# A four-stage transformer kernel on one core: the experts' low-rank product in float32r parts, keys in two transfers, and new orders on every engine

## The reference

```
x = layernorm(x + attention0(x))   # 16 heads, q and k low-rank, causal softmax
x = layernorm(x + ffn0(x))         # silu(x w1) * (x w2), gelu(h h1), gelu(h h2), w3; hidden 512
x = layernorm(x + attention1(x))   # 16 heads, no mask
x = layernorm(x + experts(x))      # below
```

```
top1 = argmax(softmax(x @ gate_W.T + gate_b))          # one of 8 experts per token
base = x @ wi_W.T + wi_b                               # 128 -> 512, shared
lora = (x @ lora_A[i].T) @ lora_B[i].T                 # 128 -> 4 -> 512, expert i
out  = sum over i of (top1 == i) * (relu(base + lora) @ wo_W.T + wo_b)
```

## Time and profile before

| | us |
|---|---|
| median of three runs | 875.84 (875.03 to 881.42) |
| the profiled execution, its own time | 876.6 |
| its span, first to last instruction | 874.5 |
| PE busy | 823.0 |
| DVE busy | 611.2 |
| ACT busy | 402.6 |
| POOL busy | 190.5 |
| mean granted clock of PE | 0.958 |

### The profile page before, as it was taken

One profiled execution on the slowest core, in us unless ns is written; L12 is line 12 of the kernel. 1 busy time (PEld: TensorE's weight loads), 2 busy tenths in 40 slices (PEclk: granted clock), 3 DMA queues, 4 the chain that ended last, 5 costly groups with the idle time before them and its releaser, 6 DMA issues.

```text
span 874.5 us, 21713 instructions
## 1 busy us (share of the span) xinstructions
PE 823.0 (94%) x8690; PEld 626.7 (72%) x8690; DVE 611.2 (70%) x1715; ACT 402.6 (46%) x823; POOL 190.5 (22%) x398
## 2 busy tenths in 40 slices
PE   8679999999989999999999999999999899999885
PEld 6457776777767687877778786877778677777554
DVE  3574685968668587877768786848847784847554
ACT  1323536273643736273554628182463627371441
POOL 4332421130302122131313113040211314010001
PEclk9789899999999999999999999999889999999779
DMA  6522222201330221213240302313020400111200
GB/s 217 203 85 74 85 87 76 75 27 61 119 121 4 87 73 37 82 56 106 68 153 21 128 32 65 104 50 112 4 92 15 141 4 27 55 36 46 87 9 13
DMA packets 43468, 64.19 MB, mean 73 GB/s; under 512 B 6088, under 2 KB 34088, under 8 KB 42984
## 3 DMA queue, kind: packets, MB, share of 16 engines
q1 hardware_dynamic: 41688, 57.93, 20.2%
q10 hardware_dynamic: 1680, 4.87, 1.6%
HBM read 43.41 MB, written 18.35 MB: 71 GB/s over the span
## 4 chain that ended last, share of the span: by engine, by line
PE 75%; DVE 7%; ACT 5%; DMA 4%; SPq 4%; issue 3%; POOL 2%; POOLq 0%; DVEq 0%; ACTq 0%
PE banks L1116 25%; PE banks L1065 10%; PE banks L1098 6%; PE banks L1172 6%; PE banks L976 5%; PE banks L1032 5%; ACT prob L618 3%; DVE top L741 3%; PE banks L943 3%; PE banks L1145 3%; DMA krow<-scratch 2%; PE banks L1077 2%; SPq L480 2%; PE banks L952 2%; PE banks L1047 2%
## 5 line engine op out<-in xcount | busy, mean ns | idle before, releaser
L741 DVE TENSOR_REDUCE top<-banks 128x3 f32<-128x384 f32 (+1 forms) x512 | 290.0, 613 | 72.7 <-PE banks L983 50.4
L618 ACT ACTIVATE prob<-banks 128x384 f32<-128x384 f32 (+1 forms) x512 | 242.0, 560 | 91.6 <-PE banks L1040 43.1
L632 ACT ACTIVATE hid<-banks 128x512 f32<-128x512 f32 x64 | 38.1, 597 | 237.0 <-PE banks L1116 237.0
L555 POOL TENSOR_TENSOR ln_rstd<-ln_var,minus_half 128x2 f32<-128x2 f32 x64 | 44.5, 701 | 439.7 <-DVE ln_var L820 439.4
L1065 PE MATMUL banks<-prob,v 128*32 128x256 f32 (+1 forms) x2048 | 122.0, 373 | 7.7 <-POOL prob L562 4.6
L1116 PE MATMUL banks<-glu,wh 128*128 128x256 f32 x512 | 120.3, 389 | 0.0
L1116 PE MATMUL banks<-hid,wh 128*128 128x256 f32 x512 | 119.3, 387 | 0.1
L1116 PEld LDWEIGHTS banks<-glu,wh 128*128 128x128 f32 x512 | 96.7, 194 | 15.6 <-issue 1.0
L1116 PEld LDWEIGHTS banks<-hid,wh 128*128 128x128 f32 x512 | 96.1, 193 | 13.9 <-DVE top L741 0.4
L1065 PEld LDWEIGHTS banks<-prob,v 128*32 128x32 f32 x2048 | 59.3, 113 | 53.0 <-issue 11.5
L976 PE MATMUL banks<-krow,qrow 32*128 32x256 f32 (+1 forms) x992 | 76.9, 336 | 14.8 <-DMA krow<-scratch 10.8
(11 more groups left out here) (110 smaller groups left out, 1027.1 us busy)
## 6 DMA issues: line engine op xcount, KB each, us to landing
scratch<-split SPq DMA_DIRECT2D x124, 128.0 KB, 2.2
qrow<-scratch SPq DMA_DIRECT2D x31, 512.0 KB, 3.6
krow<-scratch SPq DMA_DIRECT2D x124, 128.0 KB, 3.2
xt<-in_xt SPq DMA_DIRECT2D x16, 128.0 KB, 2.6
wh<-in_wh ACTq DMA_DIRECT2D x2, 1024.0 KB, 7.7
out<-xout SPq DMA_DIRECT2D x16, 128.0 KB, 2.1
x<-in_x SPq DMA_DIRECT2D x15, 128.0 KB, 3.0
prob<-in_qk_a SPq DMA_DIRECT2D x2, 512.0 KB, 4.9
```

The source lines that it names most:

```text
L555: nc.gpsimd.tensor_tensor(ln_rstd[s][:], ln_var[s][:], minus_half[:], ALU.pow).then_inc(rstd[s], 1)
L618: nc.scalar.activation(prob[s][:, j % 2, g, 0:wide], banks[:, b, 0:wide], ACT.Exp, scale=1.0 / float(np.sqrt(np.float32(HD))) if s == A0 e ...
L632: nc.scalar.activation(hid[layer][:, 2 * m:2 * m + 2, :].rearrange("p m t -> p (m t)"), banks[:, g, :], ACT.Gelu).then_inc(gelued, 1)
L741: nc.vector.tensor_reduce(out=top[s][:, :, h], in_=banks[:, b, 0:blocks * wide].rearrange("p (q k) -> p q k", q=blocks), axis=AX, op=ALU.m ...
```

## The change

Six edits; the line numbers behind `route` shift by up to 13 in the new file.

1. The low-rank product: `low` now holds, for each tile of 128 tokens, 4 x 32 columns. DVE rounds the 32 columns to float32r (`low_parts[0]`), takes the rest (`low_parts[1]`), and writes both masked, twice over. lora_B is loaded four times and made into parts as well (once, in chunk 0's route): `wlb` is its float32r value on rows 0 to 63 and the rest on rows 64 to 127. One float32r product over 128 rows then gives all four products of parts.
2. `exp_full` counts pairs of hidden blocks, and ACT's relu waits per pair.
3. The keys of a fetch come in two transfers of 256 KB, each writing a row twice, instead of four of 128 KB.
4. The last `late` step waits for `folded` (its landing place is one that the start uses), and loads lora_B four times.
5. POOL no longer clears `low`.
6. `SEQUENCE` of all five engines and `BANK_TABLE` are new.

```diff
-        NSPREAD = (1 + PARTS * PARTS) * DMA
+        NSPREAD = (1 + PARTS) * DMA
...
-        NWEIGHTS = 8 * DMA
+        NWEIGHTS = (6 + PARTS * PARTS) * DMA
         NSCALED = 5
+        ROUTED = 9
...
-                for i in range(PARTS):
-                    for k in range(PARTS):
-                        sp.dma_start(krow[s][n % DEEP[s]][PARTS * i + k::PARTS * PARTS].bitcast(F32).rearrange("p j t -> p (j t)"),
-                                     scratch[s][n % 2][1, :, k]).then_inc(there, DMA)
+                for k in range(PARTS):
+                    sp.dma_start(krow[s][n % DEEP[s]][k::PARTS].bitcast(F32).rearrange("p j t -> p (j t)"),
+                                 scratch[s][n % 2][1, :, k].unsqueeze(1).to_broadcast([GROUP * HD, PARTS, GROUPS * TOK])).then_inc(there, DMA)
...
+                    act.wait_ge(folded, 2)
                     for dst, name in ((wq[A1][:], "qk_w1"), (wv[A1][:], "v_w1"), (wo[A1][:], "o_w1"), (wi[:], "wi"), (wgl[:], "gl"),
-                                      (wlb[0:ER], "lb"), (wlb[ER:2 * ER], "lb"), (wout[:], "wo")):
+                                      *((lbraw[i * ER:(i + 1) * ER], "lb") for i in range(PARTS * PARTS)), (wout[:], "wo")):
...
-                act.wait_ge(exp_full, 1 * n + 1)
                 for pair, g in enumerate((ga, gb)):
+                    act.wait_ge(exp_full, PAIRS * n + pair + 1)
...
+                if is_first(n):
+                    dve.wait_ge(weights, NWEIGHTS)
+                    nc.vector.tensor_copy(wlb[:], lbraw).then_inc(lb_parts, 1)
+                    dve.wait_ge(lb_parts, 1)
+                    at = slice(PARTS * ER, P)
+                    nc.vector.tensor_tensor(wlb[at], lbraw[at], wlb[at].bitcast(F32), ALU.subtract).then_inc(lb_parts, 1)
...
+                nc.vector.tensor_copy(low_parts[:, :, 0].bitcast(F32R), src[:, :, EXPERTS:]).then_inc(routed, 1)
+                step(2, nc.vector.tensor_tensor(logit[:], src[:, :, 0:EXPERTS], row("gate_b").unsqueeze(1).to_broadcast(wide), ALU.add))
+                nc.vector.tensor_tensor(low_parts[:, :, 1], src[:, :, EXPERTS:], low_parts[:, :, 0], ALU.subtract).then_inc(routed, 1)
...
+                step(8, nc.vector.tensor_tensor(chosen[:].rearrange("p t (e r) -> p t e r", r=LORA), pick[:].unsqueeze(3).to_broadcast(wider),
+                                                first[:].unsqueeze(2).unsqueeze(3).to_broadcast(wider), ALU.is_equal))
+
+                for k in range(PARTS):
+                    done = nc.vector.tensor_tensor(low[:, :, k].rearrange("p t (i c) -> p t i c", i=PARTS), low_parts[:],
+                                                   chosen[:].unsqueeze(2).to_broadcast([P, TILES, PARTS, ER]), ALU.mult)
...
-                for i in range(2):
-                    for pair, g in enumerate((ga, gb)):
-                        m, tile = 2 * pair + i, slice(pair * ER, (pair + 1) * ER)
-                        done = nc.tensor.matmul(banks[:, g, i * TOK:(i + 1) * TOK], wlb[tile, m * P:(m + 1) * P], lowt[tile],
+                if is_first(n):
+                    pe.wait_ge(lb_parts, PARTS)
+                for pair, g in enumerate((ga, gb)):
+                    for i in range(2):
+                        m = 2 * pair + i
+                        done = nc.tensor.matmul(banks[:, g, i * TOK:(i + 1) * TOK], wlb[:, m * P:(m + 1) * P], lowt[:],
                                                 start=False, stop=True, skip_group_check=True)
-                done.then_inc(exp_full, 1)
+                    done.then_inc(exp_full, 1)
```

More of the change, by code:

```diff
@@ L338, in build @@
         first = sb("first", [P, TILES])
-        low = sb("low", [P, TILES, P])
-        lowt = sb("lowt", [P, TOK])
+        low = sb("low", [P, TILES, PARTS, PARTS * ER])
+        low_parts = sb("low_parts", [P, TILES, PARTS, ER])
+        chosen = sb("chosen", [P, TILES, ER])
+        lowt = sb("lowt", [P, TOK], F32R)
         scratch = {s: [nc.dram_tensor(f"scratch{s}_{i}", [2, GROUP * HD, PARTS, GROUPS * TOK], F32, kind="Internal").ap() for i in range(2)]
@@ L529, in _ @@
                     nc.gpsimd.memset(top[s][:].rearrange("p q h -> p (q h)"), 0.0)
-            nc.gpsimd.memset(low[:].rearrange("p t c -> p (t c)"), 0.0).then_inc(blank, 1)
-            pool.wait_ge(blank, 3)
+            pool.wait_ge(blank, 2)
             nc.gpsimd.memset(ones[:].bitcast(F32), 1.0).then_inc(ones_made, 1)
@@ L851, in route @@
                 dve.wait_ge(route_full, 1 * n + 1)
-                step(1, nc.vector.tensor_tensor(logit[:], src[:, :, 0:EXPERTS], row("gate_b").unsqueeze(1).to_broadcast(wide), ALU.add))
-                step(2, nc.vector.tensor_reduce(out=best[:], in_=logit[:], axis=AX, op=ALU.max))
-                step(3, nc.vector.tensor_tensor(pick[:], logit[:], best[:].unsqueeze(2).to_broadcast(wide), ALU.is_ge))
-                step(4, nc.vector.tensor_tensor(pick[:], pick[:], ranks[:].unsqueeze(1).to_broadcast(wide), ALU.mult))
@@ L857, in route @@
-                step(5, nc.vector.tensor_reduce(out=first[:], in_=pick[:], axis=AX, op=ALU.min))
-                step(6, nc.vector.tensor_tensor(pick[:], pick[:], first[:].unsqueeze(2).to_broadcast(wide), ALU.is_equal))
-                for i in range(2):
-                    done = nc.vector.tensor_tensor(low[:, :, i * ER:(i + 1) * ER].rearrange("p t (e r) -> p t e r", r=LORA),
-                                                   src[:, :, EXPERTS:].rearrange("p t (e r) -> p t e r", r=LORA),
-                                                   pick[:].unsqueeze(3).to_broadcast([P, TILES, EXPERTS, LORA]), ALU.mult)
+                nc.vector.tensor_copy(low_parts[:, :, 0].bitcast(F32R), src[:, :, EXPERTS:]).then_inc(routed, 1)
@@ new lines, in route @@
+                step(2, nc.vector.tensor_tensor(logit[:], src[:, :, 0:EXPERTS], row("gate_b").unsqueeze(1).to_broadcast(wide), ALU.add))
+                nc.vector.tensor_tensor(low_parts[:, :, 1], src[:, :, EXPERTS:], low_parts[:, :, 0], ALU.subtract).then_inc(routed, 1)
+                step(4, nc.vector.tensor_reduce(out=best[:], in_=logit[:], axis=AX, op=ALU.max))
+                step(5, nc.vector.tensor_tensor(pick[:], logit[:], best[:].unsqueeze(2).to_broadcast(wide), ALU.is_ge))
+                step(6, nc.vector.tensor_tensor(pick[:], pick[:], ranks[:].unsqueeze(1).to_broadcast(wide), ALU.mult))
@@ new lines, in route @@
+                step(7, nc.vector.tensor_reduce(out=first[:], in_=pick[:], axis=AX, op=ALU.min))
+                wider = [P, TILES, EXPERTS, LORA]
+                step(8, nc.vector.tensor_tensor(chosen[:].rearrange("p t (e r) -> p t e r", r=LORA), pick[:].unsqueeze(3).to_broadcast(wider),
[3 more added lines that the diff above has]
+                                                   chosen[:].unsqueeze(2).to_broadcast([P, TILES, PARTS, ER]), ALU.mult)
```

99 lines of the change are left out of this document (50 added, 49 removed).

## The result

| | before | the change |
|---|---|---|
| median, us | 878.63 (875.03 to 881.78, 4 runs) | 829.5 (824.0 to 831.24, 4 runs) |
| ratio, 95% interval | | 0.9431 [0.9366, 0.9497] |
| profiled execution, span | 876.6, 874.5 | 828.5, 826.8 |
| mean granted clock | 0.958 | 0.974 |

The change takes 49 us off, where 15 were forecast and the range ended at 847. The comparisons leave disturbed runs out.

The account below looks back on a forecast made before the run. PE was taken to bound the middle, waits for keys the head, a chain through all engines the end. -4.7 - 2 + 1.5 - 14.5 + 4.8 = -14.9 against 876.6 gave 861.5 us, range 847 to 877.

Parts of the forecast that it names:

- the order in the middle: Middle: key spacing tighter, most chunks just make it, two or three wait 1 to 3 us; +1.5 us, -10 to +20.
- Product: Experts' low-rank product on PE: 0.43 us saved per chunk, eleven experts ahead of the last F0 work; -4.7 us.
- Work moved from the middle to the end: PE steps that go behind chunk 15's F0 down, out of the full middle: -14.5 us.
- End: Behind chunk 15's F0 down: 75 us long instead of 70.2, with more DVE work; +4.8 us, 0 to +17.4.
- the rival in which the end gives the gain back: DVE becomes the end's bound, the end is 87.6 us long and the time 874; chance 0.17.
- Head: Start: chunk 1's keys 4 to 5 us earlier, chunk 2's late beside the weights; -2 us, -6 to +3.
- Keys in two transfers: SP's key fetches: two fewer issues bring the last landing forward 1.2 us, if 256 KB lands about as fast.
- more than forecast: Wider spacings of maxima and lora take a third off the middle's waits, the end stays at 72: 850 us; chance 0.15.
- The sign set for the middle: Middle: the forecast would be wrong if PE's busy time there was not lower by about 19 us.

Follow-up runs that it names:

- the orders alone: The kernel before with the new SEQUENCE and BANK_TABLE and nothing else: 839.26 us, ratio 0.9548.
- second head version: The change with wh and w3 after five exps, late weights behind chunk 2's keys, scales and w12 ahead of chunk 1's split: 825.1 us.
- second profiled execution: The changed kernel run again, unedited, for comparison on the same chip: 828.04 us, ratio 0.9415.
- delayed exps: An idle one-column exp on ACT ahead of the first and third exp of each four: kernel before 890.58 us, the change 833.6 us.

## Why the prediction was wrong

The step that failed is **"the order in the middle"**, priced at +1.5 us between -10 and +20; it measured -34.6. Point by point:

- *Product:* -4.7 forecast, -4.3 measured in the middle (8 us in all with what goes with it). Right in size, and in part by luck: the matmuls themselves save 0.22 us per expert and not 0.43, and a pause of 0.28 in front of them, which the working did not have, makes up for it.
- *Work moved from the middle to the end:* -14.5 forecast. With the orders alone the middle's work fell from 698.9 to 685.2 by the ledger, that is 13.7. Right.
- *End:* +4.8 forecast, +3.3 measured. Right in size; it began at 753 instead of 784, for the reason below. DVE was busy 52.66 of 73.6 us there, so the rival in which the end gives the gain back did not happen. Whether the DVE steps named in the forecast are what made the end longer, no run takes apart.
- *Head:* -2 forecast, +1.9 measured, inside the bounds. The exchange of waits is as described (keys of chunk 2 with a wait of 4.07 us), but chunk 1's keys came at 33.3, not near 30: with the scales and w12 beside the x load and the parking, the parking landed at 27.34 us instead of 22.27, 5.1 later and not 2. The second head version, with the scales earlier, has the keys at 30.1.
- *Keys in two transfers:* the condition "if a 256 KB transfer lands about as fast" does not hold (4.3 against 3.2 us); the effect is nil.
- *Order in the middle:* the working looked at one wait only, the keys, and found that "most chunks then just make it". That came true: behind 51 us no wait for keys in the middle is over 1 us (one of 1.44 in the second profiled execution). But keys were some 4.5 of the 56.5 us of excess in the middle before. The rest was short waits for ACT and the mask, in no row that I had read, and I carried it over unchanged into a kernel in which every step had a new place. It fell by 20.6 us. And I priced the clock as 1.7 us on one wait of 2.38, though the middle had 20.5 us of it before; 14.0 of them went together with the waits.
- *The rival "more than forecast"* named this and gave it a third of 37 us, chance 0.15. Excess in the middle fell by 61%. Its own sum was off: a third of 37 is 12.3, and with the end at 72 instead of 75 that gives 846 at most, not 850, already below the range's end of 847. Its reason, wider spacings, is only half right: on maxima they are wider and it shows, on ACT's answers they are not, and there the gain is fewer misses.
- *The range:* with the product at -4.7, the lowest values that the forecast allows its five terms add up to -35, that is 841. The range stopped at 847, and even 841 would have been too high, because the middle's term ended at -10.

The sign set for the middle was PE's busy time lower by about 19 us. It fell by 41 (733.99 to 692.86): 18.5 of that is work and 14.0 the clock's part, since half-speed time counts as busy. The other 8.6 are short waits that the busy time does not show, because in the profile a wait before a weight load can pass while the matmul before it still counts as busy.

Still open is what in the new orders makes the hits more frequent. No single group of steps was moved alone, since an engine's list can't be cut without the others, and the order of the steps was not told apart from the new bank table. Fewer waits and a higher clock come together in the traces with the new orders; that the one is the cause of the other was not tested, and in the change the delayed exps brought back 4.4 us of plain waits and only 0.3 of the clock's part.

## What to carry to other kernels

When every engine's order is new, none of the old waits may be carried over. Add up all that PE takes beyond its steps at full clock, short waits and half-speed stretches together, and treat the sum as what the new order may keep or remove: here 56 us, of which two fifths remained. A delay test tells slack from luck: two orders can be equally tight, and one of them still waits half as often. And one repaired wait proves little on a kernel whose clock falls now and then: the position of the steps behind it shows the local gain, and only several executions show what is left of it at the end.

## What the runs showed of the hardware

- One wait alone does not tell whether half speed follows. The same 0.85 us wait was followed by full speed in one kernel and by half speed in another (above). In the nine profiled executions with the new orders (15 to 20 us of plain waits in a middle of 702 to 709) there is no stretch at 0.50 between 68 and 760 us, even with ACT's answers delayed; in each of the five with the old ones (33 to 41 us in 753 to 768) there are 31 to 51 us of it there. The page's clock rows (tenths, in 40 slices; a 9 is full speed) of the kernel before, of it with delayed exps, of the change, and of the change with delayed exps:

```profile
PEclk9789899999999999999999999999889999999779
```

```profile
PEclk9788999999999999999899999999699798999788
```

```profile
PEclk9769999999999999999999999999999999999799
```

```profile
PEclk9669999999999999999999999999999999999899
```

- Four float32r matmuls of 256 columns over 128 rows start 0.12 us apart behind the second, float32 pairs on two groups of 32 rows 0.21 apart. In both, 0.31 us lie between the first and the second start. The float32r ones begin 0.03 us behind the last start of the float32 product in front of them, the float32 pairs 0.31 us.
- A key transfer of 256 KB, which writes every row twice, landed 1.1 us later after its issue than one of 128 KB (4.3 against 3.2), about the 1.2 us of the two issues on SP that it saves.
- A load of x (128 KB) on SP's queue landed 7.3 us after its issue beside the scales on ACT's queue, and 3.0 us after it without them.
